# The key transposes of causal linear attention, at the start of the next eighth of a unit instead of the end of their own

## The chip, the cores and the metric

One Trainium2 chip, one of its cores. The metric is the device time of one execution in microseconds, the median of the runs. The program is one launch with three phases behind each other: the attention phase (with the token mixing ahead of it), an MLP phase with the router, and a phase of routed experts.

## What is computed

The reference takes x of 16 x 512 x 256 x 4. Cut to what matters here:

```
h = einsum('bhid,oi,od->bho', x, weighted_sum, weight)      # token mixing
z = layernorm(h)
# attention on z, 16 heads of 64, causal and linear:
q, k = elu((ln(z) @ wq) @ proj) + 1, elu((ln(z) @ wk) @ proj) + 1;  v = ln(z) @ wv
for t: kv += k_t v_t^T; ksum += k_t; out_t = (q_t kv) / (q_t ksum + 1e-6)
z = z + out @ wo;  z = z + gelu(ln(z) @ w1 + b1) @ w2 + b2;  h = h + z
h = h + mixture_of_experts(layernorm(h))                     # 8 routed, 1 shared
```

The change touches only the scan over t, in the attention phase.

## The kernel before

Each of the 16 images has 512 tokens. They are worked on in two **units** of 256 tokens, and each unit in two **chunks** of 128 tokens (`c` from 0 to 3 over an image). A chunk takes four **eighths** of a unit, one for each group `g` of four heads; an eighth is called by its number `s` from 0 to 7, and `s` 0 to 3 are chunk 2h, 4 to 7 chunk 2h + 1 of half h. All matrix products are done in two halves of fp16 (a high part and the rest), which is why so many steps come as "make the high part, then the low part".

Causal attention is done by chunks: within a chunk the scores of 128 x 128 are made, masked and multiplied with the values (`scores`, `scores_split`, `outputs`); over the chunks before, the running sum `kvacc` of k v^T is used (`kvh`, `kvl`). To add a chunk to that sum its keys must be turned, with the token on the partition. This is the step `keys(i, c, part)`, with `part` 0 and 1 for eight heads each. It runs for chunks 0 to 2; chunk 3 is the last and its sum is not needed.

- On TensorE `keys` is eight transposes (L645) from `ks` into the PSUM bank `pT`.
- On VectorE it is one copy (L917) of `pT` into `kt`, 128 x 1024 fp16.
- The other engines have nothing to do in it, and it issues no DMA.

The same bank `pT` takes the transposes of the attention's output, step `turn` (L705), four transposes that ScalarE then copies to `ot` (L803). The uses of `pT` follow each other strictly: each waits on the semaphore `turn_read` until the one before has been copied out. For chunk c the order is keys part 0, `turn` of group 0, keys part 1, `turn` of groups 1, 2, 3. `sums(i, c, g)` (L691, L692) multiplies `kt` with the values, and VectorE adds the result to `kvacc`.

There is no scheduler. One function `run`, called once for each engine with that engine's own steps, goes through the same list of steps, and each engine takes from it what it has. So the order of the calls in `unit` is the order on every engine. An eighth is made of: `outputs` of its group; the `turn` of an earlier group; the `scores` of a later one; and blocks of dense work from the table `DENSE`, of which the `early` ones stand ahead of `outputs` and the `late` ones behind it. A dense block "f" is eight heads' features (L550 to L552 into `pF`, then ScalarE's two activations L775 and L779, VectorE's `z` L876 and `hi` L881, GpSimd's `lo` L972, which together are the step `phi`), "v" a block of values (`vh` L785 on ScalarE, `vl` L886 on VectorE), "p" the output projection. At `s` = 2 the steps `x0` and `normed` of the unit after the next stand at the beginning: on VectorE L852, two of L863 and two `nl` (L869), on ScalarE L761 and L766; TensorE has no part in them. The last two units have no such unit ahead.

In the kernel before, `keys` of part 0 is called in eighth g = 1 behind `sums`, and part 1 in eighth g = 2, also behind `sums`, both ahead of `scores_split` (VectorE's `sl`, L909, in odd eighths) and ahead of the late `phi`.

Of the kernel before, what the change touches and what calls it, by code (L numbers as in the profile page):

```python
# [24 lines left out]
CH = 4  # L25
# [39 lines left out]
def after(u, n):  # L65

    return u[0] + (u[1] + n) // 2, (u[1] + n) % 2
# [27 lines left out]
def attention_phase(nc, io, w1_w, w2_w, mlp_loaded):  # L95
# [4 lines left out]
    with ExitStack() as ctx:  # L100
# [228 lines left out]
        def run(engine, steps):  # L329


            def step(name, *args):
                if name in steps:
                    steps[name](*args)

            def use(u, what, bank, before):


                kind, n = what
                if kind == "p":  # L340
                    step("project", after(u, -1), bank, before)
                elif kind == "f":
                    step("features", after(u, 1), n, bank, before)
                else:
                    step("values", after(u, 1), n, bank, before)

            def finish(u, what, bank):
                if what[0] == "f":
                    step("phi", after(u, 1), what[1], bank)
                elif what[0] == "p":  # L350
                    step("project_read", after(u, -1), bank)
                    step("residual", after(u, -1))

            def real(u):
                return u[0] < SEQS

            def mixed(u, k):
                step("mix", u, k)
                if k == XS - 1:
                    step("h", u)  # L360

            def normed(u):
                step("mean", u)
                step("centre", u)
                step("var", u)
                step("rstd", u)
                step("x0", u)
                step("normed", u)

            def dense(turn, first, last):  # L370


                slots, n = [], turn % 2
                before = {n: ("v", VALS - 2, 1), 1 - n: ("v", VALS - 1, 1)}
                for s in range(8):
                    uses = [], []
                    for place, (kind, k) in enumerate(DENSE[s]):
                        if not ((kind == "p" and first) or (kind != "p" and last)):
                            uses[place].append(((kind, k), n % 2, before[n % 2]))
                            before[n % 2] = (kind, k, 0)  # L380
                        n += 1
                    slots.append(uses)
                return slots

            def unit(u, start=False, last=False):


                i, h = u
                slots = dense(h, start, last)
                ahead, far = after(u, 2), after(u, 3)  # L390
                for s in range(8):
                    c, g = 2 * h + s // 4, s % 4
                    early, late = slots[s]

                    summed = (c, g - 2) if g >= 2 and c < CH - 1 else (c - 1, g + 2) if g < 2 and c > 0 else None

                    if g < 2:
                        quad = (i, c, g + 2)
                    elif c < CH - 1:
                        quad = (i, c + 1, g - 2)  # L400
                    else:
                        quad = None if last else (i + 1, 0, g - 2)
                    if s == 2 and real(ahead):
                        step("x0", ahead)
                        step("normed", ahead)
                    for what in early:
                        use(u, *what)
                    step("outputs", i, c, g)

                    if g >= 2:  # L410
                        step("turn", i, c, g - 2)
                    elif c > 0:
                        step("turn", i, c - 1, g + 2)
                    elif not start:
                        step("turn", i - 1, CH - 1, g + 2)
                    for what in early:
                        finish(u, *what[:2])
                    if quad is not None:
                        step("scores", *quad)
                    step("outputs_split", i, c, g)  # L420
                    if s == 1 and real(ahead):
                        step("var", ahead)
                        step("rstd", ahead)
                    for what in late:
                        use(u, *what)
                    if summed is not None:
                        step("sums", i, *summed)
                    if g in (1, 2) and c < CH - 1:
                        step("keys", i, c, g - 1)
                    if quad is not None:  # L430
                        step("scores_split", *quad)
                    if summed is not None:
                        step("sums_split", i, *summed)
                    if s == 0 and real(ahead):
                        step("mean", ahead)
                        step("centre", ahead)
                    if 1 <= s <= XS and real(far):
                        step("split", far, s - 1)
                    if s >= 4 and real(far):
                        mixed(far, s - 4)  # L440
                    for what in late:
                        finish(u, *what[:2])

            for k in range(XS):
                step("split", (0, 0), k)
                mixed((0, 0), k)
            normed((0, 0))
            for k in range(XS):
                step("split", (0, 1), k)
            slots = dense(-1, True, False)  # L450
            for s in range(8):
                for what, bank_no, before in slots[s][0] + slots[s][1]:
                    use((0, -1), what, bank_no, before)
                    finish((0, -1), what, bank_no)
                if s < XS:
                    mixed((0, 1), s)
                elif s == 4:
                    normed((0, 1))
            for k in range(XS):
                step("split", (1, 0), k)  # L460
                mixed((1, 0), k)
            for q in range(2):
                step("scores", 0, 0, q)
                step("scores_split", 0, 0, q)
            unit((0, 0), start=True)
            unit((0, 1))
            for i in range(1, SEQS - 1):
                unit((i, 0))
                unit((i, 1))
            unit((SEQS - 1, 0))  # L470
            unit((SEQS - 1, 1), last=True)
            step("turn", SEQS - 1, CH - 1, 2)
            step("turn", SEQS - 1, CH - 1, 3)
            step("project", (SEQS - 1, 1), LAST_BANK, ("p", 0, 1))
            step("project_read", (SEQS - 1, 1), LAST_BANK)
            step("residual", (SEQS - 1, 1))
# [1721 lines left out]
```

## Time and profile before

| | us |
|---|---|
| median of 3 runs | 2622.9 (2621.56 to 2630.17) |
| the profiled execution | 2629.9 |
| its span | 2628.2 |
| TensorE busy | 2258.0 (86%) |
| VectorE busy | 1783.4 (68%) |
| ScalarE busy | 1525.8 (58%) |
| GpSimd busy | 1468.2 (56%) |
| mean granted clock of TensorE | 0.946 of full |

The span is the profiled execution's own, from its first to its last instruction. Busy time is the time in which at least one instruction of the engine runs. The attention phase takes the first 1500 us or so. Matmuls overlap in the rows, so a matmul's duration is more than the distance to the next one: a row of 0.27 us may stand 0.11 us behind the last.

### The profile page before, as it was taken

How to read it: one execution, taken by the hardware profiler on the slowest of the kernel's cores; microseconds unless marked ns; L12 is line 12 of the kernel's file. 1: busy time of each engine (PE TensorE's matmuls, PEld its weight loads, DVE VectorE, ACT ScalarE, POOL GpSimd, SP SyncE). 2: the span in 40 equal slices, each digit the busy share in tenths (PEclk: the TensorE clock that was granted, in tenths of full speed). 3: DMA queues.
4: the chain of work that ended last, by engine and by line, in shares of the span. 5: the costliest groups of instructions: out<-in, count | busy, mean ns of one | idle time of the engine just before them, and what ended most of it. 6: DMA issues, size and time to landing. Idle time of an engine off the chain costs nothing. (4 is left out here: it accounts for less than half of the span.)

```text
span 2628.2 us, 64033 instructions
## 1 busy us (share of the span) xinstructions
PE 2258.0 (86%) x24112; PEld 1738.2 (66%) x24112; DVE 1783.4 (68%) x3983; ACT 1525.8 (58%) x2890; POOL 1468.2 (56%) x1449
## 2 busy tenths in 40 slices
PE   3799999999999999999999858989998999894774
PEld 2588787878787887878787736555555555552553
DVE  2477778777777777777777746766776677664442
ACT  3576777767777777677677645544554455441232
POOL 1376666666666756666666621553454345436576
PEclk8899999999999999999999979999999999997887
DMA  3344444444444434444443330111111111000775
GB/s 109 101 129 126 108 123 128 123 117 123 125 116 123 115 97 114 100 105 105 114 102 90 82 107 33 57 52 54 42 57 66 40 35 46 27 21 17 156 141 71
DMA packets 310913, 236.32 MB, mean 90 GB/s; under 512 B 28057, under 2 KB 275853, under 8 KB 310608
## 3 DMA queue, kind: packets, MB, share of 16 engines
q1 hardware_dynamic: 274352, 197.25, 28.1%
q0 software_dynamic: 23808, 21.74, 4.7%
q10 hardware_dynamic: 12448, 13.24, 1.6%
q8 instruction: 194, 3.18, 0.5%
q14 instruction: 111, 0.91, 0.1%
HBM read 73.32 MB, written 82.58 MB: 59 GB/s over the span
## 5 line engine op out<-in xcount | busy, mean ns | idle before, releaser
L1857 POOL DMA_INDIRECT slot_dram<-xt,slot_u x256 | 267.4, 1045 | 77.1 <-issue 77.1
L550 PE MATMUL pF<-nh,qk_h 128*128 128x256 f16 x1024 | 281.7, 275 | 7.8 <-DVE nl L869 4.4
L551 PE MATMUL pF<-nh,qk_l 128*128 128x256 f16 x1024 | 281.5, 275 | 0.0
L552 PE MATMUL pF<-nl,qk_h 128*128 128x256 f16 x1024 | 281.3, 275 | 0.0
L972 POOL TENSOR_TENSOR lo<-z,hi 128x512 f16<-128x512 f32 x128 | 148.6, 1161 | 198.6 <-DVE hi L881 198.6
L1845 POOL TENSOR_TENSOR xt<-xn,xt 128x512 f16<-128x512 f32 x32 | 40.0, 1269 | 330.5 <-ACT xt L1528 330.5
L796 ACT ACTIVATE sh<-sm 128x512 f16<-128x512 f32 x256 | 160.0, 625 | 88.2 <-DVE sm L902 82.5
L984 POOL TENSOR_TENSOR ol<-on,oh 128x256 f16<-128x256 f32 x256 | 172.2, 673 | 69.5 <-ACT oh L819 69.5
L876 DVE SCALAR_TENSOR_TENSOR z<-pF,z 128x512 f32<-128x512 f32 x256 | 175.1, 684 | 41.6 <-ACT z L779 39.0
L972 POOL TENSOR_TENSOR w_w<-z,hi 128x512 f16<-128x512 f32 x128 | 157.7, 1232 | 60.4 <-DVE hi L881 60.4
L991 POOL TENSOR_TENSOR kvl<-kvacc,kvh 128x260 f16<-128x260 f32 x192 | 157.9, 822 | 50.3 <-ACT kvh L827 50.3
L902 DVE TENSOR_TENSOR sm<-pS,mask 128x512 f32<-128x512 f32 x256 | 174.4, 681 | 10.1 <-PE pS L636 10.1
L1309 PE MATMUL pY<-w_h,gh 128*128 128x256 f16 x512 | 154.5, 302 | 30.0 <-issue 29.8
L550 PE MATMUL pO<-vh,sh 128*128 128x65 f16 x1024 | 119.4, 193 | 67.7 <-issue 48.1
L881 DVE CAST hi<-z 128x512 f16<-128x512 f32 x256 | 170.5, 666 | 8.8
L775 ACT ACTIVATE z<-pF 128x512 f32<-128x512 f32 x256 | 149.9, 586 | 45.1 <-PE pF L552 42.9
L966 POOL TENSOR_TENSOR xl<-w_w,xh 128x512 f16<-128x512 f32 x128 | 148.0, 1159 | 47.3 <-ACT xh L726 47.3
L1311 PE MATMUL pY<-w_l,gh 128*128 128x256 f16 x512 | 154.1, 301 | 22.4 <-issue 22.0
L1310 PE MATMUL pY<-w_h,gl 128*128 128x256 f16 x512 | 154.6, 302 | 18.6 <-issue 18.4
L803 ACT ACTIVATE ot<-pT 128x512 f16<-128x512 f16 x256 | 149.8, 585 | 31.0 <-PE pT L705 30.3
L779 ACT ACTIVATE z<-z 128x512 f32<-128x512 f32 x256 | 161.3, 630 | 8.2
L2107 POOL DMA_INDIRECT out_rows<-yb,xg x80 | 126.7, 1584 | 61.4 <-ACT yb L2052 35.9
(299 smaller groups left out, 8517.1 us busy)
## 6 DMA issues: line engine op xcount, KB each, us to landing
w_w<-in_x SPq DMA_DIRECT2D x128, 256.0 KB, 3.0
qdh<-hi SPq DMA_DIRECT2D x256, 128.0 KB, 2.7
qdl<-lo SPq DMA_DIRECT2D x256, 128.0 KB, 2.8
ks<-hi SPq DMA_DIRECT2D x128, 128.0 KB, 3.1
ks<-w_w SPq DMA_DIRECT2D x128, 128.0 KB, 3.1
slot_dram<-blank ACTq DMA_DIRECT2D x8, 1360.0 KB, 6.7
xg<-slot_dram SPq DMA_DIRECT2D x40, 272.0 KB, 2.9
x_dram<-x SPq DMA_DIRECT2D x32, 256.0 KB, 2.2
```

The source lines that it names most:

```text
L550: pe.matmul(out, wh, mh, start=first, stop=False, skip_group_check=True)
L551: pe.matmul(out, wl, mh, start=False, stop=False, skip_group_check=True)
L552: return pe.matmul(out, wh, ml, start=False, stop=last, skip_group_check=True)
L779: nc.scalar.activation(z[:, s, :, :], z[:, s, :, :], ACT.Exp, scale=-1.0, bias=-math.log(PHI_DOWN)).then_inc(e_ready, 1)
L796: nc.scalar.activation(sh[:, q, :, :], sm[:, n % 2, :, :], ACT.Copy).then_inc(sh_ready, 1)
L876: nc.vector.scalar_tensor_tensor(z[:, s, :, :], pF[bank_no][:, :].rearrange("p (b n) -> p b n", b=2), 0.0, z[:, s, :, :], ALU.max, ALU.add ...
L881: nc.vector.tensor_copy(hi[:, n % MOVES, :, :], z[:, s, :, :]).then_inc(fh_ready, 1)
L902: nc.vector.tensor_tensor(sm[:, n % 2, :, :], pS[:, :].rearrange("p (a b) -> p a b", b=P), mask[:, :].unsqueeze(1).broadcast_to([P, 4, P]) ...
L972: nc.gpsimd.tensor_tensor(lo[n % MOVES // 2][:, n % 2, :, :], z[:, units(w, FEATS, n) % ZS, :, :], hi[:, n % MOVES, :, :], ALU.subtract).t ...
L984: nc.gpsimd.tensor_tensor(ol[:, n % 2, :], on[:, n % 2, :, :].rearrange("p a b -> p (a b)"), oh[:, n % 2, :], ALU.subtract).then_inc(ol_re ...
L991: nc.gpsimd.tensor_tensor(kvl[:, heads, :], kvacc[:, heads, :], kvh[:, heads, :], ALU.subtract).then_inc(kvl_ready, 1)
L1857: nc.gpsimd.indirect_dma_start(io["slot_dram"], bass.IndirectOffsetOnAxis(slot_u[:, i % XT, c, k:k + 1], 0), xt[:, i % XT, c, :], None, bo ...
```

## The change

The two calls of `keys` move. Part 0, called at the end of eighth g = 1, is now called at the beginning of eighth g = 2, and part 1 at the beginning of g = 3 instead of the end of g = 2. In both cases the new place is behind `x0` and `normed`, where these are called.

```diff
                     if s == 2 and real(ahead):
                         step("x0", ahead)
                         step("normed", ahead)
+
+                    if g >= 2 and c < CH - 1:
+                        step("keys", i, c, g - 2)
                     for what in early:
                         use(u, *what)
                     step("outputs", i, c, g)
...
                     if summed is not None:
                         step("sums", i, *summed)
-                    if g in (1, 2) and c < CH - 1:
-                        step("keys", i, c, g - 1)
                     if quad is not None:
                         step("scores_split", *quad)
```

The order of the uses of `pT` stays as it was, and so do all semaphore counts. Lines behind the second place are one higher in the changed file (L917 becomes L918, L705 becomes L706).

VectorE's queue, at the end of eighth 1 and the first part of eighth 2 of a unit in the middle, before:

```order
L917 COPY kt<-pT 128x1024 [waits kv_done,turned]
L909 TENSOR_TENSOR sl<-sm,sh 128x512 [waits sh_ready]
L876 SCALAR_TENSOR_TENSOR z<-pF,z 128x512 [waits e_ready]
L881 CAST hi<-z 128x512 [waits moved_k,f_ready]
L852 TENSOR_TENSOR x<-w_w 128x512 [waits x1_stored,hx_ready1,xc_ready,rs_step]
L863 SCALAR_TENSOR_TENSOR w_w<-x,g,r 128x256 [waits nh_ready,nl_ready,x0_ready,rs_step]
L863 SCALAR_TENSOR_TENSOR w_w<-x,g,r 128x256
L869 SCALAR_TENSOR_TENSOR nl<-w_w,b,nh 128x256 [waits nh_ready,tn_ready] x2
L926 TENSOR_SCALAR dn<-pO 128x4 [waits o_done]
```

and after the change:

```order
L910 TENSOR_TENSOR sl<-sm,sh 128x512 [waits sh_ready]
L877 SCALAR_TENSOR_TENSOR z<-pF,z 128x512 [waits e_ready]
L882 CAST hi<-z 128x512 [waits moved_k,f_ready]
L853 TENSOR_TENSOR x<-w_w 128x512 [waits x1_stored,hx_ready1,xc_ready,rs_step]
L864 SCALAR_TENSOR_TENSOR w_w<-x,g,r 128x256 [waits nh_ready,nl_ready,x0_ready,rs_step]
L864 SCALAR_TENSOR_TENSOR w_w<-x,g,r 128x256
L870 SCALAR_TENSOR_TENSOR nl<-w_w,b,nh 128x256 [waits nh_ready,tn_ready] x2
L918 COPY kt<-pT 128x1024 [waits kv_done,turned]
L927 TENSOR_SCALAR dn<-pO 128x4 [waits o_done]
```

The copy `kt` of part 0 has moved past seven other instructions, from ahead of `sl` to behind `nl`.

The same queue at the end of eighth 2 and the start of eighth 3, before:

```order
L947 COPY kvacc<-pKV 128x260 [waits kvl_ready,kvh_ready,kv_done]
L917 COPY kt<-pT 128x1024 [waits kv_done,turned]
L876 SCALAR_TENSOR_TENSOR z<-pF,z 128x512 [waits e_ready]
L881 CAST hi<-z 128x512 [waits moved_k,f_ready]
L886 SCALAR_TENSOR_TENSOR vl<-pF,vh 128x8x64 [waits vh_ready]
```

and after the change:

```order
L948 COPY kvacc<-pKV 128x260 [waits kvl_ready,kvh_ready,kv_done]
L877 SCALAR_TENSOR_TENSOR z<-pF,z 128x512 [waits e_ready]
L882 CAST hi<-z 128x512 [waits moved_k,f_ready]
L918 COPY kt<-pT 128x1024 [waits kv_done,turned]
L887 SCALAR_TENSOR_TENSOR vl<-pF,vh 128x8x64 [waits vh_ready]
```

The copy of part 1 has moved behind the late feature block's `z` and `hi`.

And VectorE's queue at the end of eighth 5 and the start of eighth 6, in chunk 1 of an image, before:

```order
L917 COPY kt<-pT 128x1024 [waits kv_done,turned]
L909 TENSOR_TENSOR sl<-sm,sh 128x512 [waits sh_ready]
L876 SCALAR_TENSOR_TENSOR z<-pF,z 128x512 [waits e_ready]
L881 CAST hi<-z 128x512 [waits moved_k,f_ready]
L926 TENSOR_SCALAR dn<-pO 128x4 [waits o_done]
```

and after the change:

```order
L910 TENSOR_TENSOR sl<-sm,sh 128x512 [waits sh_ready]
L877 SCALAR_TENSOR_TENSOR z<-pF,z 128x512 [waits e_ready]
L882 CAST hi<-z 128x512 [waits moved_k,f_ready]
L918 COPY kt<-pT 128x1024 [waits kv_done,turned]
L927 TENSOR_SCALAR dn<-pO 128x4 [waits o_done]
```

Here it has moved behind `sl`, `z` and `hi`.

On TensorE the transposes keep their place between the same matmuls, except in eighths 5 and 6 of a unit with chunks 0 and 1: there the twelve matmuls of a step of token mixing (`mix`, L550 to L552 into `pM`), which stood behind the transposes, now stand ahead of them.

## Rows read from the trace of the kernel before

**Rows 1.** Busy time by engine (instructions), granted clock, DMA share, GB/s, steady part.
```profile
core 0: us, PE busy (x) PEld busy (x) DVE busy (x) ACT busy (x) POOL busy (x), PEclk, DMA share, GB/s
400.00:1400.00 1000.00, 931.93 (x12423) 798.17 (x12422) 773.68 (x1601) 710.73 (x1444) 659.42 (x691) 1.00 0.44 114
```
**Rows 2.** TensorE's waits, 400 to 1400 us: for whom, us in total, times, longest.
```profile
PE pO L550 <- issue: 35.4, 23, 1.8
PE pT L645 <- ACT ot L803: 24.6, 22, 1.5
PE pO L550 <- DVE sl L909: 7.1, 22, 0.7
```
**Rows 3.** Timeline of TensorE: start us, us, line, out<-in, count [idle before <-releaser].
```profile
711.67 0.27 PE L705 MATMUL pT<-ident,oh 128*128 128x128 f16 x2
...
713.54 0.27 PE L552 MATMUL pF<-nl,qk_h 128*128 128x256 f16 x1
...
715.20 0.62 PE L645 MATMUL pT<-ident,ks 128*128 128x128 f16 x8 [1.14 <-ACT ot L803]
715.85 0.39 PE L550 MATMUL pF<-wv_h,nh 128*128 128x512 f16 x1
...
717.89 0.27 PE L705 MATMUL pT<-ident,oh 128*128 128x128 f16 x2
...
719.63 0.38 PE L552 MATMUL pF<-wv_l,nh 128*128 128x512 f16 x1
...
723.38 0.19 PE L550 MATMUL pO<-vh,sh 128*128 128x65 f16 x1 [1.44 <-issue]
```
**Rows 4.** Timeline of VectorE in the same unit.
```profile
705.90 0.69 DVE L917 COPY kt<-pT 128x1024 f16<-128x1024 f16 x1
708.34 0.69 DVE L909 TENSOR_TENSOR sl<-sm,sh 128x512 f16<-128x512 f32 x1 [1.74 <-ACT sh L796]
...
713.57 0.88 DVE L869 SCALAR_TENSOR_TENSOR nl<-w_w,b,nh 128x256 f16<-128x256 f32 x2 [0.31 <-ACT nh L761]
714.37 0.15 DVE L926 TENSOR_SCALAR dn<-pO 128x4 f32<-128x4 f32 x1
...
717.24 0.68 DVE L876 SCALAR_TENSOR_TENSOR z<-pF,z 128x512 f32<-128x512 f32 x1
717.96 1.23 DVE L881 CAST hi<-z 128x512 f16<-128x512 f32 x1
...
721.50 0.69 DVE L886 SCALAR_TENSOR_TENSOR vl<-pF,vh 128x512 f16<-128x512 f32 x1 [0.37 <-ACT vh L785]
```
**Rows 5.** The tile `kt`: min/median/max ns, first and last start.
```profile
L917 DVE COPY kt<-pT x96: 672/682/693, 120.3 to 1512.3; 128x1024 f16<-128x1024 f16 x96
```
**Rows 6.** Timeline of ScalarE in the same unit.
```profile
714.57 0.58 ACT L803 ACTIVATE ot<-pT 128x512 f16<-128x512 f16 x1
...
715.55 0.58 ACT L775 ACTIVATE z<-pF 128x512 f32<-128x512 f32 x1
716.16 0.63 ACT L779 ACTIVATE z<-z 128x512 f32<-128x512 f32 x1
```
**Rows 7.** Timeline of VectorE in the unit before, eighths 5 to 7.
```profile
686.35 1.02 DVE L909 TENSOR_TENSOR sl<-sm,sh 128x512 f16<-128x512 f32 x1
...
688.01 0.43 DVE L881 CAST hi<-z 128x512 f16<-128x512 f32 x1
688.35 0.16 DVE L926 TENSOR_SCALAR dn<-pO 128x4 f32<-128x4 f32 x1
...
694.06 0.69 DVE L886 SCALAR_TENSOR_TENSOR vl<-pF,vh 128x512 f16<-128x512 f32 x1 [1.67 <-ACT vh L785]
```
**Rows 8.** Timeline of TensorE in that unit, eighth 6.
```profile
687.97 0.27 PE L705 MATMUL pT<-ident,oh 128*128 128x128 f16 x2
```
**Rows 9.** TensorE after a long wait, and the busy time behind it.
```profile
123.41 0.19 PE L550 MATMUL pO<-vh,sh 128*128 128x65 f16 x1 [3.12 <-DVE sl L909]
123.50:126.90 3.40, 3.40 (x32) 2.96 (x32) 3.23 (x5) 0.34 (x1) 2.26 (x2) 0.50 0.85 195
```

## The prediction

> **What bounds the kernel now.** The first view to read is the busy time of each engine over the steady part of the attention phase. From 400 to 1400 us TensorE is busy 932 of 1000 us at a granted clock of 1.00; VectorE has 774, ScalarE 711, GpSimd 659 [rows 1]. So TensorE is the bound, with some 68 us per 1000 of idle time, and what matters is what stops it. The waits of TensorE in the same window name it: 22 waits before the key transposes (L645) for ScalarE's copy `ot`, 24.6 us; 23 before the first score-times-value matmul (L550, `pO`), 35.4 us, which the view can't attribute; and 22 short ones for `sl` [rows 2]. That is one of each large kind in every unit (half image; 22 or 23 units lie in the window). Everything I forecast is per unit, so one unit is replayed: the one whose eighth 1 ends at 705 us.
>
> TensorE's rows there [rows 3]: the output transposes at 711.67, the eighth's feature matmuls end at 713.81 (713.54 + 0.27), then after the sums 1.14 us of idle until the key transposes of part 1 at 715.20; value matmuls at 715.85; the next output transposes at 717.89; the last value matmul of eighth 3 ends at 720.01 (719.63 + 0.38); 1.44 us idle before 723.38.
>
> VectorE's rows [rows 4]: the copy `kt` (part 0) at 705.90, 0.69 us. Behind it VectorE is idle 1.74 us, until ScalarE has made `sh`, and only then `sl` starts at 708.34. From there it runs nearly solid: the normalisation of a later unit ends with two `nl` from 713.57 (0.88 us, up to 714.45), `dn` at 714.37, then, with `kt` of part 1 just ahead of it, `z` 717.24, `hi` 717.96, `vl` 721.50. So before `sl` VectorE has time to give away, and from 708.34 to 723 it has hardly any. That decides the case.
>
> **The change, part by part.** It adds and removes no instruction: 768 transposes and 96 `kt` copies stay. No DMA is issued by the step, and SP, ScalarE and GpSimd have no part in it, so their queues keep their order. What moves is the place in the queues of TensorE and VectorE.
>
> On TensorE the place is the same at the boundary of eighths 1 and 2 and of 2 and 3: nothing of TensorE stands between the end of one eighth and the start of the next. Only in eighths 5 and 6 (chunk 1 of an image) twelve mixing matmuls come ahead of the transposes instead of behind them. They are work either way: cost nil.
>
> On VectorE `kt` moves much further. It goes behind `sl`, the late `phi` pair (`z`, `hi`), and, at eighth 2, behind the whole of `x0` and `normed`, which are called ahead of the new place. And TensorE's next output transposes wait for that copy, since they write the same bank `pT`: there is a queue of one between them.
>
> *Step 1, `kt` of part 0 at eighth 2.* Taking it from 705.90 frees 0.69 us where VectorE then idles 1.74 us for `sh` [rows 4], so `sl` stays at 708.34 and the rest of that chain too: gain nil. It now stands where `dn` stood, at 714.37, and ends 0.68 to 0.69 later, 715.06 (the 96 copies took 0.672 to 0.693 us [rows 5]). TensorE reaches the output transposes at 711.67, as now, and gets them at 715.1: **a new wait of 3.4 us**. Behind them on TensorE, which issues in order, stand the scores, a feature block, the sums, the key transposes and the values.
>
> *Step 2, the old wait goes.* TensorE is through with the sums 1.14 us ahead of 715.20, at 714.06, 2.39 us behind the start of the output transposes, so the key transposes of part 1 come at 715.1 + 2.4 = 717.5. By then ScalarE has long copied `ot`: its own normalisation ends where `ot` began, 714.57 [rows 6], and the copy takes 0.58 from the end of the transposes at 715.5. The wait of 1.14 us disappears; TensorE is at 717.5 against 715.20, 2.3 us late.
>
> *Step 3, `kt` of part 1 at eighth 3.* Now it stands behind `z` and `hi` of the late feature block. That block ends 2.14 us after the output transposes (711.67 to 713.81), at 717.2. ScalarE's two activations take 0.58 and 0.63 [rows 6], so 718.5; `z` on VectorE 0.72 until `hi` may start (717.24 to 717.96 [rows 4]), 719.3; `hi` takes 1.23 us at this place [rows 4] but 0.43 in a quieter one [rows 7]. `kt` then ends between 720.5 and 721.2. Values follow the key transposes by 0.65 and the output transposes follow the values by 2.04 [rows 3], so TensorE stands ready at 717.5 + 0.65 + 2.04 = 720.2 and waits 0.3 to 1.0 us more. I take 721.2, by the row of the very same `hi`, since GpSimd's `sl`, whose neighbour `hi` is, waits for ScalarE as `hi` does and moves with it. Against 717.89 TensorE is 3.3 us late (2.5 with the short `hi`: 720.4).
>
> *Step 4, up to the next rendezvous.* The last value matmul ends 2.12 us behind the output transposes (717.89 to 720.01), so 723.3; ScalarE's `vh`, as large as its `z`, takes 0.58 [rows 6] and `vl` follows, 723.95 against 721.50 now. From `vl` to the matmul at 723.38 is 1.88 us [rows 3, 4], so that one comes at 725.85: **2.5 us late**, 1.7 with the short `hi`. TensorE's own work gives less (5.49 us from 717.89 to 723.38 less 1.44 idle is 4.05; 721.2 + 4.05 = 725.25), so this chain is the last. Behind it VectorE has gaps again and nothing makes up for the delay.
>
> The normalisation stands in eighth 2 of 30 of the 32 units (the last two have none ahead): 30 x 2.5 = **75 us**, at the low end 30 x 1.7 = 51.
>
> *Step 5, chunk 1 of each image (eighths 5 to 7).* At eighth 6 `kt` takes the place of `dn`, 688.35, right behind `hi` [rows 7], and ends at 689.04; TensorE was at the output transposes at 687.97 [rows 8]: 1.1 us of wait. What VectorE can gain by the removed copy is the time in which `sl` followed it, between 0 and some 0.6 us (`sl` at 686.35 [rows 7]); at eighth 1 `sl` waits for ScalarE's `sh` anyway, so I take little, 0.15, and the wait as 0.95 us, 16 times: **15 us**, with 0.5 x 16 = 8 and 1.1 x 16 = 18 as ends. TensorE has no wait for the rest of this unit in which the delay could be made good. The second `kt` of the chunk falls where VectorE idles 1.67 us (`vl` at 694.06 [rows 7]): nil.
>
> *Step 6, TensorE's clock.* The steady part runs at 1.00 with waits of up to 1.8 us [rows 1, 2]. The trace has one wait near the new length: 3.12 us that ended at 123.41, and in the 3.4 us behind it the granted clock was 0.50, that is 1.2 GHz [rows 9]. The new wait is 3.4 us. Behind it stand the 2.1 us of scores and features on which step 3 hangs. 3.4 us at half rate do 1.7 us of work less. From both sides: nothing if the clock stays, 1.7 per unit if it falls every time once, up to 2.1 if all the work ahead of `z` runs at half rate. I take 1.5, nearer to the one row that has such a wait: 30 x 1.5 = **45 us**, ends 0 and 63.
>
> One page was weighed for step 1. The nearest row for a VectorE copy that moves among GpSimd's work is `hi`, 0.43 against 1.23 us [rows 4, 7]; the `kt` copies lie between 0.672 and 0.693 wherever they stand [rows 5]. The Trainium skill, page "VectorE: DVE Perf Modes", section "Why PSUM operands drop a tier", says that a copy out of PSUM can't use both SBUF read ports, and its section "Two Vector instructions with no wait between them" that the second of these is shared with GpSimd; by that, `kt`, which reads PSUM, does not swell, and the trace agrees (0.69). Were it to swell like `hi`, step 1 would be 0.8 us longer per unit, 24 us in all.
>
> **The sum.** 75 + 15 + 45 = 135 us. The profiled execution took 2629.9 us with a span of 2628.2, so it would become 2765; the median of the runs is 2622.9, 7 lower, and the forecast for it is 2622.9 + 135, some **2758 us**.
>
> **The rivals.**
> (a) The waits come, the clock holds. For it: it never left 1.00 in the steady part. Against it: [rows 9]. 90 us more, 2713.
> (b) The clock falls for twice as long, since the waits of steps 3 and 4 follow some 6 and 11 us behind: 30 x 3 for step 6, 2803. For it: nothing in the steady part shows how fast it comes back after a second wait.
> (c) Hidden. VectorE reaches `kt` in time because the chain ahead of it starts 0.6 us earlier without the old copy. The 1.74 us of idle before `sl` speak against it, and 0.6 would not cover 3.4. 2623.
> (d) Faster. The old wait for `ot` (1.14 us, 32 times, 36 us) goes and no new one comes, 2587. That needs `kt` to end by 711.67, that is the normalisation 3.4 us earlier; a gain begins only once the new wait is below 1.1 us. `x0` and the normalisation sit behind `hi` and ScalarE, neither of which changes.
> (e) The change doesn't move `kt` past `normed`: excluded by the order of the built program, which has it between `nl` and `dn`.
>
> **How the numbers follow.** Forecast 0.57, (a) 0.22, (b) 0.13, (c) 0.05, (d) 0.03. The range: the low end takes (a) with the low ends of step 4 and 5, halfway, 2695 (75 down to 51 and 15 down to 8 would make 2682); the high end leaves the far half of (b), 2795. Within 0.3% of 2622.9 is about what a measurement of this kernel can't tell from no change; (c) is that case, 0.05, (d) the faster one, 0.03, and the rest, 0.92, is slower.
>
> **What would show each step.** In the changed kernel's waits of TensorE a new group stands on top: output transposes (one line on, L706) for `kt`, some 30 of 3.4 us, 30 near 1.0 and 16 near 1.0, about 150 us in all, and the group "key transposes for `ot`" is gone. VectorE idles longer before `sl` at eighth 1 (2.3 us). The granted clock from 400 to 1400 us is below 1.00, near 0.95; if it is 1.00, step 6 is wrong and (a) holds. If the time from one image to the next grows by 5.6 us (90 / 16) where the clock holds, steps 1 to 5 are right. I am wrong if `kt` at eighth 2 doesn't start right behind `nl`, or if the wait at 723.38 absorbs more than the 0.8 us of the delay that step 4 lets it (3.3 down to 2.5).

## Result and profile after

The changed kernel takes 2762.1 us (median of 4 runs, 2756.33 to 2763.01), the kernel before 2622.9: the ratio is 1.052, with a 95% interval of 1.0496 to 1.0544, so it is 139 us slower. The forecast was 2758. One of the four runs of the kernel with `nh` and `nl` around eighth 7 took 12801 us and is left out of its numbers below.

The runs of this study were made in groups, on several chips, and the kernel before took 2622.9, 2610.3 or 2502.5 to 2502.9 us in them; each comparison below is with the kernel before in the same group. This difference between groups lies behind the attention phase, so one more number is used that compares all of them: the start of the first scatter of the MLP phase (GpSimd's first write of `slot_dram`), which is the end of the attention phase plus a stretch that the change doesn't touch. It stands at 1647.3 us before and 1781.9 us after, so 134.6 us are made in the attention phase. Behind it the two profiled executions differ the other way, 980.9 us before and 972.7 after; the profiled executions took 2629.9 us, near the top of that kernel's runs, and 2756.3, the lowest of the other's (2765 was forecast for it). In a second profile of the changed kernel, in another group, the scatter stands at 1781.8. The rows are those of the tile `slot_dram` (min/median/max ns, first and last start), before and after:

```profile
L1857 POOL DMA_INDIRECT slot_dram<-xt,slot_u x256: 978/981/1383, 1647.3 to 2424.5; - x128
```
```profile
L1858 POOL DMA_INDIRECT slot_dram<-xt,slot_u x256: 978/980/1383, 1781.9 to 2552.5; - x128
```

The busy time of the engines in the steady part, after (columns as in [rows 1]), and TensorE's waits there (as [rows 2]):

```profile
core 0: us, PE busy (x) PEld busy (x) DVE busy (x) ACT busy (x) POOL busy (x), PEclk, DMA share, GB/s
400.00:1400.00 1000.00, 880.37 (x11333) 749.88 (x11332) 712.74 (x1458) 652.87 (x1313) 597.41 (x626) 0.97 0.40 104
```
```profile
PE pT L706 <- DVE kt L918: 100.9, 50, 3.6
PE pO L551 <- issue: 11.7, 20, 0.6
PE pO L551 <- DVE sl L910: 7.0, 21, 0.7
```

TensorE has 120 us of idle time per 1000 instead of 68, and its clock has left 1.00. The wait for `ot` [rows 2] is gone, and the unattributed one fell from 35.4 to 11.7 us. In their place stand 50 waits of the output transposes for `kt`, 100.9 us. Over the whole run they are 78 waits and 153.4 us, where the prediction had some 76 and 150.

One unit of the changed kernel in which the clock held, TensorE (timeline, columns as in [rows 3]):

```profile
771.54 0.28 PE L706 MATMUL pT<-ident,oh 128*128 128x128 f16 x2 [3.27 <-DVE kt L918]
...
773.42 0.27 PE L553 MATMUL pF<-nl,qk_h 128*128 128x256 f16 x1
...
773.78 0.61 PE L646 MATMUL pT<-ident,ks 128*128 128x128 f16 x8
...
777.69 0.29 PE L706 MATMUL pT<-ident,oh 128*128 128x128 f16 x2 [1.27 <-DVE kt L918]
...
782.33 0.19 PE L551 MATMUL pO<-vh,sh 128*128 128x65 f16 x1 [0.59 <-issue]
```

and VectorE beside it, which answers to [rows 4]:

```profile
764.77 0.69 DVE L910 TENSOR_TENSOR sl<-sm,sh 128x512 f16<-128x512 f32 x1 [2.44 <-ACT sh L797]
...
770.00 0.88 DVE L870 SCALAR_TENSOR_TENSOR nl<-w_w,b,nh 128x256 f16<-128x256 f32 x2 [0.31 <-ACT nh L762]
770.80 0.68 DVE L918 COPY kt<-pT 128x1024 f16<-128x1024 f16 x1
...
775.02 0.69 DVE L877 SCALAR_TENSOR_TENSOR z<-pF,z 128x512 f32<-128x512 f32 x1 [0.62 <-ACT z L780]
775.75 1.28 DVE L882 CAST hi<-z 128x512 f16<-128x512 f32 x1
776.95 0.68 DVE L918 COPY kt<-pT 128x1024 f16<-128x1024 f16 x1
777.55 0.68 DVE L887 SCALAR_TENSOR_TENSOR vl<-pF,vh 128x512 f16<-128x512 f32 x1
```

Read the two together. `kt` of part 0 starts at 770.80, right behind the `nl` pair, ends at 771.48, and TensorE goes on at 771.54 after 3.27 us. The idle time before `sl` grew from 1.74 to 2.44 us: the 0.7 us that the old copy took there were given away for nothing. The second `kt` ends at 777.63, TensorE goes on at 777.69 after 1.27 us. The key transposes (773.78) wait for nobody now.

### The profile page after: what moved, and what is told of

It is laid out like the page before. It is cut to its first block and busy times, and to the rows that moved or that the text cites. A ratio compares the mean times of both kernels' runs of the same rounds, so it can differ in the third digit from the quotient of the medians.

```text
span 2754.6 us, 64033 instructions
## 1 busy us (share of the span) xinstructions
PE 2299.7 (83%) x24112; PEld 1768.9 (64%) x24112; DVE 1795.4 (65%) x3983; ACT 1534.4 (56%) x2890; POOL 1467.7 (53%) x1449
## 5 line engine op out<-in xcount | busy, mean ns | idle before, releaser
L551 PE MATMUL pF<-nh,qk_h 128*128 128x256 f16 x1024 | 292.4, 286 | 8.6 <-DVE nl L870 4.4
L552 PE MATMUL pF<-nh,qk_l 128*128 128x256 f16 x1024 | 291.7, 285 | 0.0
L553 PE MATMUL pF<-nl,qk_h 128*128 128x256 f16 x1024 | 291.3, 284 | 0.0
L706 PE MATMUL pT<-ident,oh 128*128 128x128 f16 x512 | 73.7, 227 | 155.0 <-DVE kt L918 153.4
L979 POOL TENSOR_TENSOR sl<-sm,sh 128x512 f16<-128x512 f32 x128 | 148.3, 1158 | 69.8 <-ACT sh L797 69.6
L910 DVE TENSOR_TENSOR sl<-sm,sh 128x512 f16<-128x512 f32 x128 | 104.4, 816 | 106.0 <-ACT sh L797 106.0
L967 POOL TENSOR_TENSOR xl<-w_w,xh 128x512 f16<-128x512 f32 x128 | 147.7, 1157 | 47.4 <-ACT xh L727 47.4
```

The source lines that it names most:

```text
L551: pe.matmul(out, wh, mh, start=first, stop=False, skip_group_check=True)
L552: pe.matmul(out, wl, mh, start=False, stop=False, skip_group_check=True)
L553: return pe.matmul(out, wh, ml, start=False, stop=last, skip_group_check=True)
```

## Experiments

Each kernel is an edit of `unit`'s list of steps or of one engine's steps. "Scatter" is the start of the first scatter less 1647.3. The time from one image to the next is the distance of two like waits of TensorE some 90 us apart, near 700 to 900 us; where the clock falls it varies by a microsecond or so.

| kernel | ratio to before (95%) | us over before | scatter | image to image |
|---|---|---|---|---|
| before | 1 | 0 | 0 | 90.04 |
| changed | 1.052 (1.0496 to 1.0544) | +139 | +134.6 | 98.28, 99.35 |
| changed, again | 1.0518 (1.0501 to 1.0536) | +135.2 | +134.5 | |
| part 0 alone | 1.0398 (1.0381 to 1.0416) | +101.0 | +101.3 | 97.11 |
| part 1 alone | 1.0024 (1.0013 to 1.0035) | +5.3 | +4.4 | 90.08 |
| ahead of x0 and normed | 1.0158 (1.0142 to 1.0175) | +39.8 | +39.0 | 92.30 |
| changed, wait filled | 1.0396 (1.0379 to 1.0414) | +98.6 | +100.3 | 96.41 |
| changed, chunk 1 as before | 1.0435 (1.0418 to 1.0453) | +113.4 | +110.8 | 97.49 |
| before, normed at eighth 4 | 1.0126 (1.0109 to 1.0143) | +33.3 | +32.7 | 92.26 |
| before, x0 and normed at 4 | 1.0195 (1.0178 to 1.0212) | +51.7 | +49.8 | 93.35 |
| before, nh and nl around eighth 7 | 1.0246 (1.0223 to 1.0269) | +62.0 | +60.7 | 93.47 |
| before, all but x0 at eighth 7 | 1.0314 (1.0293 to 1.0336) | +81.1 | +79.2 | 95.41 |
| before, L863 at eighths 5 and 7 | 1.0242 (1.0223 to 1.0261) | +62.5 | +63.4 | 94.76 |
| before, nh and nl at start of eighth 7 | **0.9898** (0.9881 to 0.9914) | **-25.6** | -24.6 | 88.12 |

### Part 0 alone

```diff
                         step("normed", ahead)
+                    if g == 2 and c < CH - 1:
+                        step("keys", i, c, 0)
...
-                    if g in (1, 2) and c < CH - 1:
-                        step("keys", i, c, g - 1)
+                    if g == 2 and c < CH - 1:
+                        step("keys", i, c, 1)
```

> Only part 0 of the key transposes is moved to the start of the next eighth; part 1 stays at the end of its own. My theory (the copy kt stands behind the normalisation on VectorE, TensorE's output transposes wait for it): the wait of 3.3 us at eighth 2 stays whole, the ones at eighth 3 go, because kt of part 1 falls where VectorE waits for ScalarE. By the same replay as in the prediction the unit is 1.3 us late instead of 2.5, so 30 x 1.3 + 15 + 45 for the clock = 99 us over the kernel before, about 2722, and the clock still falls once in most units. Rival (each of the two moves costs by its own, half each): 2692.

Measured: 2603.6 against 2502.5, 101 us more; expected were 99. TensorE's waits from 400 to 1400 us:

```profile
PE pT L707 <- DVE kt L919: 78.0, 31, 3.6
```

31 waits instead of 50: the 3.3 us ones and those of chunk 1 are left, those at eighth 3 are gone. The granted clock there is 0.97, as in the changed kernel. Part 0 alone makes three quarters of the loss.

### Part 1 alone

```diff
                         step("normed", ahead)
+                    if g == 3 and c < CH - 1:
+                        step("keys", i, c, 1)
...
-                    if g in (1, 2) and c < CH - 1:
-                        step("keys", i, c, g - 1)
+                    if g == 1 and c < CH - 1:
+                        step("keys", i, c, 0)
```

> Only part 1 is moved. My theory: no wait of 3 us anywhere, so the clock stays at 1.00 in the steady part and the old wait for ot stays too, now at the start of eighth 3. kt of part 1 stands behind hi, TensorE waits 0.9 to 1.9 us for it, and VectorE's own chain, which has the same work in it, gives most of it back by the next wait: 0 to 1.1 us per unit, 2623 to 2656, I take 2641. Rival (half each): 2692.

Measured: 5.3 us more, at the low end of the 0 to 33 expected. The waits:

```profile
PE pT L647 <- ACT ot L805: 24.5, 22, 1.5
PE pT L707 <- DVE kt L919: 19.8, 23, 1.0
PE pO L552 <- issue: 13.6, 23, 0.8
```

The wait for `ot` is where it was [rows 2], a wait for `kt` of 0.67 to 1.03 us is new, and the one behind it fell from 35.4 to 13.6 us: what TensorE loses at eighth 3 it gets back at eighth 4, since VectorE's queue has the same work in it up to there. The two moves together cost 139 us, the sum of the two alone is 106: behind a late part 0, part 1 has no such slack.

### Both, ahead of x0 and normed

```diff
+                    if g >= 2 and c < CH - 1:
+                        step("keys", i, c, g - 2)
                     if s == 2 and real(ahead):
                         step("x0", ahead)
                         step("normed", ahead)
-
-                    if g >= 2 and c < CH - 1:
-                        step("keys", i, c, g - 2)
```

> Both parts at the start of the next eighth, but called ahead of x0 and normed instead of behind them. On TensorE this is the very same order as the changed kernel. My theory: kt of part 0 then ends at about 711.6 in the replayed unit, when TensorE reaches the output transposes at 711.67, so the wait of 3.3 us goes and with it the falls of the clock; left are the waits at eighths 3 and 6. 30 x (0.5 to 1.3) + 15 = 30 to 54 us over before, about 2665. Rival (the cost comes from where TensorE's transposes stand, or from the mixing matmuls that they changed places with): no different from the changed kernel, 2762.

Measured: 39.8 us more (expected 30 to 54). TensorE has the very order of the changed kernel, and 99 us of the 139 are gone. So it is not the place of the transposes on TensorE that costs; it is that `kt` stands behind the normalisation on VectorE.

```profile
PE pT L646 <- ACT ot L804: 36.3, 22, 2.0
PE pT L706 <- DVE kt L918: 28.4, 32, 1.0
PE pO L551 <- issue: 12.9, 22, 0.6
```

No wait is longer than 2 us, and the granted clock from 400 to 1400 us is 1.00 to two places; it fell once, behind a wait of 1.99 us (rows in the last section).

### The wait filled with matmuls

The output's values are not touched: the fillers write columns that nobody reads.

```diff
+FILL = 28
...
                     step("outputs", i, c, g)
+                    if s == 2 and real(ahead):
+                        step("fill", i, c, g)
...
+            def fill(i, c, g):
+                for k in range(FILL):
+                    pe.matmul(pKV[:, 4 * VW:512], qk_h[:, 0, 0:P], qk_l[:, 0, 0:512 - 4 * VW], start=True, stop=True,
+                              skip_group_check=True)
```

> The changed kernel with 28 more matmuls of 252 columns, into columns of a PSUM bank that nobody reads, right ahead of the output transposes of eighth 2 (30 units). They are 3.0 us of work and fit into the wait of 3.3 us, so they add nothing by themselves; they keep TensorE busy. If step 6 of the prediction holds (the falls of the clock cost some 45 of the 139 us), the clock stays at 1.00 from 400 to 1400 us and the time is about 2717. If the clock's falls cost nothing, since TensorE waits for others anyway, it stays at 2762; if the fillers are in the way, above that.

```profile
702.19 3.17 PE L689 MATMUL pKV<-qk_l,qk_h 128*128 128x252 f16 x28
705.66 0.29 PE L714 MATMUL pT<-ident,oh 128*128 128x128 f16 x2 [0.29 <-DVE kt L926]
```
```profile
400.00:1400.00 1000.00, 935.11 (x12181) 802.29 (x12182) 729.61 (x1495) 671.13 (x1352) 614.26 (x643) 1.00 0.42 106
```

Measured: 98.6 us over before, where the changed kernel is 135 to 139. The 28 matmuls fill the wait to 0.29 us and add nothing; the clock is back at 1.00. By the start of the scatter the difference is 134.6 - 100.3 = 34 us: that is what the clock's falls behind these waits cost, shown by a kernel that does more work and is faster.

### The changed kernel again, and with chunk 1 as before

```diff
-                    if g >= 2 and c < CH - 1:
+                    if g >= 2 and c in (0, 2):
                         step("keys", i, c, g - 2)
...
                         step("sums", i, *summed)
+                    if g in (1, 2) and c == 1:
+                        step("keys", i, c, g - 1)
```

> The changed kernel itself, beside the experiments on their own chip, where the kernel before takes some 2502 us. What stands in the attention phase is the same there, so 139 us over before, about 2641. If it is less by some 40, the clock's falls (which the fillers took away in the experiment before) are not the same on this chip.

> The changed kernel, but with the key transposes of chunk 1 of every image where they were (end of their own eighth); chunks 0 and 2 stay moved. Step 5 of the prediction: 15 us less than the changed kernel, since the wait of 0.97 us at eighth 6 goes, 16 times. Rival: another wait of that half takes its place, 0 us less.

Measured: 135.2 us over before for the changed kernel, 113.4 for the other, 21.8 us less where 15 were expected. The next section measures the step itself at 1.1 us an image, 18 us. The other 4 us are not shown to have a cause; the clock falls at other places in this kernel (mean 0.97 in both).

### Moving the normalisation instead

All experiments so far say that VectorE's queue of eighths 2 and 3 is what TensorE waits for. If so, taking the normalisation out of it should make the kernel before faster. The first attempt moved `normed` from eighth 2 to eighth 4:

```diff
                     if s == 2 and real(ahead):
                         step("x0", ahead)
+                    if s == 4 and real(ahead):
                         step("normed", ahead)
```

> The kernel before, with normed of the later unit called at the start of eighth 4 instead of eighth 2 (x0 stays). It touches no key transpose. If it is the normalisation on VectorE and ScalarE that makes the chain of eighths 2 and 3 late, both waits of the kernel before (1.14 us for ot, 1.44 us ahead of the first score-value matmul) go: 30 x 2.6 = 78 us faster, less what the normalisation costs at its new place, where VectorE idles some 2.2 us of the 2.5 that it needs: about 2435, 2425 to 2460. Rival: the waits come from VectorE's total work and turn up again in eighths 4 to 6: 2502.

Measured: 33 us slower, where 68 us faster were expected. Both theories were off. The two waits per unit did shrink: from the output transposes of eighth 2 to the first score-value matmul of eighth 4 TensorE takes 9.6 us (725.15 to 734.78) instead of 11.7 (711.67 to 723.38). But more came back behind it:

```profile
734.78 0.19 PE L551 MATMUL pO<-vh,sh 128*128 128x65 f16 x1 [0.89 <-issue]
739.76 0.28 PE L706 MATMUL pT<-ident,oh 128*128 128x128 f16 x2 [0.20 <-ACT ot L804]
741.06 0.23 PE L636 MATMUL pS<-qdh,ks 128*128 128x128 f16 x1 [0.90 <-DVE sm L903]
748.12 0.19 PE L551 MATMUL pO<-vh,sh 128*128 128x65 f16 x1 [1.84 <-DVE sl L910]
```

From 734.78 to 748.12 are 13.34 us; the same stretch before is 723.38 to 733.55, 10.17. VectorE's side shows why:

```profile
734.49 2.25 DVE L864 SCALAR_TENSOR_TENSOR w_w<-x,g,r 128x256 f32<-128x256 f32 x2
736.67 0.47 DVE L870 SCALAR_TENSOR_TENSOR nl<-w_w,b,nh 128x256 f16<-128x256 f32 x1
737.39 0.48 DVE L870 SCALAR_TENSOR_TENSOR nl<-w_w,b,nh 128x256 f16<-128x256 f32 x1 [0.25 <-ACT nh L762]
737.79 0.15 DVE L927 TENSOR_SCALAR dn<-pO 128x4 f32<-128x4 f32 x1
```

The normalisation now stands ahead of `dn`, and takes 3.3 us there, since the pair L864 takes 2.25 us where GpSimd works beside both of them, instead of 1.59 where it works beside one. VectorE's idle time ahead of `dn` at eighth 4 was no room: it is the time that TensorE takes to make what `dn` reads, and the scores and the outputs hang on what follows.

> As the experiment with normed at eighth 4, but with x0 moved there too. Theory: the same waits are gone, and 0.7 us more of VectorE's work is put where it has 2.2 us of idle time, so it is equal to or up to 10 us slower than with normed alone: about 2440. Rival (total work): 2502.

Measured: 51.7 us slower, so 18 more for the 0.7 us of x0 in 30 units: at that place nearly all of it is on the path (30 x 0.7 = 21).

The next three put the work at eighth 7, where VectorE idles 1.85 us ahead of `vl`. For them `normed` was cut into its parts: `tn` (VectorE's two L863), `nh` (ScalarE), `nl` (VectorE) and `hb` (ScalarE's two `hT`). In each, `nl` and `hT` were called at the end of that eighth and `nh` at its start; the first left the two L863 at eighth 2, the second took them to eighth 7, the third one of them to eighth 5.

```diff
                         step("x0", ahead)
-                        step("normed", ahead)
+                        step("tn", ahead, (0, 1))
+                    if s == 7 and real(ahead):
+                        step("nh", ahead)
...
                         finish(u, *what[:2])
+                    if s == 7 and real(ahead):
+                        step("nl", ahead)
+                        step("hb", ahead)
```

> The kernel before with the last part of the normalisation (ScalarE's two nh and two hT, VectorE's two nl) taken from eighth 2 to eighth 7; the two L863 stay at eighth 2. The experiment with all of it at eighth 4 showed that VectorE's idle time ahead of dn is no room, since the score and output chain hangs on dn and sm; at eighth 7 the idle 1.7 to 1.85 us stands ahead of vl, on which nobody waits soon. Theory: ot is copied at once, the wait of 1.14 us goes, VectorE's chain is 1.1 us shorter: 30 x 1.1 = 33 us faster than the kernel before, ratio 0.987. Rival (any later place costs TensorE more than it gives, as at eighth 4): 1.00 or slower.

> The two L863 are moved to eighth 7 too; only x0 stays at eighth 2. If the gain goes on with the work that is taken out of eighth 2, 2.06 us per unit (as far as eighth 4, which the experiment with normed at eighth 4 showed) less some 0.5 us where L863 is longer than VectorE's idle 1.85 us at eighth 7: 30 x 1.5 = 45 us faster, ratio 0.983. Rival: at eighth 7 the L863 pair takes 2.25 us beside GpSimd, as it did at eighth 4, and vl comes late for eighth 0 of the next unit: between 0 and 20 us faster.

> As the one before, with the first L863 at eighth 5 and the second at eighth 7. Theory: the first one falls into 1.44 us of idle time ahead of dn, of which it takes 0.8 to 1.1, so no wait comes of it, and the second fits into eighth 7: 30 x 1.9 = 57 us faster, ratio 0.978. Rival: what is ahead of dn delays it as at eighth 4, so slower than with all at eighth 7.

Measured: 62, 81 and 62 us slower, where 33, 45 and 57 us faster were expected; the rivals failed too, but for the first one's, which had it slower. The wait for `ot` was gone, as expected, and a larger one stood at eighth 0 of the next unit. Timeline of the first of the three, VectorE and then TensorE:

```profile
766.58 0.88 DVE L882 SCALAR_TENSOR_TENSOR nl<-w_w,b,nh 128x256 f16<-128x256 f32 x2
767.56 0.27 PE L555 MATMUL pF<-nh,qk_h 128*128 128x256 f16 x1 [2.27 <-issue]
```

The matmul at 767.56 is the first of the feature block at eighth 0 of the next unit, which reads `nh` and `nl`, and the two `nl` end at 767.46. What I had overlooked is that the deadline of `nl` is the start of that eighth for TensorE, which runs ahead of VectorE; the end of eighth 7 in VectorE's queue is too late. The clock was 0.97 in all three.

That gave the last one: `nl` at the start of eighth 7, ahead of `vl`, and `hT` in ScalarE's gap of 1.4 us at eighth 3.

```diff
                         step("x0", ahead)
-                        step("normed", ahead)
+                        step("tn", ahead, (0, 1))
+                    if s == 7 and real(ahead):
+                        step("nh", ahead)
+                        step("nl", ahead)
...
                         step("turn", i - 1, CH - 1, g + 2)
+                    if s == 3 and real(ahead):
+                        step("hb", ahead)
```

> The kernel before, with nh and nl called at the start of eighth 7 (in the experiment with nl at its end TensorE stood 2.3 to 2.5 us at eighth 0 of the next unit, whose first feature block needs nl, and the clock fell there) and the two hT called in eighth 3 between ScalarE's ot and oh, where it idles 1.44 us. The two L863 stay at eighth 2. Theory: VectorE's two nl and ScalarE's nh fall into the 1.85 us in which VectorE waits ahead of vl at eighth 7, so no new wait comes; the wait of 1.14 us for ot goes and VectorE's chain of eighths 2 and 3 is 1.2 us shorter (measured with nl at the end of eighth 7: 10.5 us from the output transposes to the first score-value matmul of eighth 4, against 11.7). 30 x 1.2 = 36 us faster than the kernel before, ratio 0.986. Rival: TensorE is bound by the length of VectorE's queue as a whole and the 1.2 us come back in eighths 4 to 7 or at eighth 0: ratio 1.00 or above.

Measured: 2477.1 against 2502.7, ratio 0.9898, 25.6 us faster than the kernel before, and so faster than both kernels of this case. The steady part's waits and busy time:

```profile
PE pO L555 <- issue: 33.6, 22, 1.7
PE pO L555 <- DVE sl L926: 11.8, 22, 1.1
PE pF L555 <- DVE x L910: 2.4, 11, 0.4
```
```profile
400.00:1400.00 1000.00, 951.86 (x12731) 818.53 (x12729) 806.51 (x1634) 725.25 (x1476) 675.67 (x704) 1.00 0.45 115
```
```profile
721.43 1.78 DVE L882 SCALAR_TENSOR_TENSOR nl<-w_w,b,nh 128x256 f16<-128x256 f32 x2 [0.57 <-ACT nh L766]
723.14 0.68 DVE L903 SCALAR_TENSOR_TENSOR vl<-pF,vh 128x512 f16<-128x512 f32 x1
```

TensorE is busy 952 of 1000 us, against 932 [rows 1]. The wait for `ot` (24.6 us [rows 2]) is gone and nothing of its size has come. It is 10 us less than expected. The two `nl` take 1.78 us at eighth 7 where they took 0.88 at eighth 2 [rows 4], and the wait for `sl` grew from 7.1 to 11.8 us; that these make up the 10 us was not tested. At the end of the phase, from 1430 to 1505 us, the granted clock fell four times; before it did not fall from 170 us until 1516.

## Why the prediction was right

- **Steps 1 and 2 (part 0 behind the normalisation).** Forecast: a wait of 3.4 us, the old one of 1.14 gone. Measured: 3.13 to 3.31 us in 25 of the 29 places where it is over 3 us, the old one gone. From the output transposes to the key transposes it was 773.78 - 771.54 = 2.24 us where I had written 2.39; this lay off the path, since TensorE waits again at the next output transposes.
- **Step 3 (part 1 behind `hi`).** Forecast 0.3 to 1.0 us, 1.0 taken. Measured 1.27 (777.69), with `hi` at 1.28, and 1.64 in the units of the other kind (told under step 4), which the replay of one unit did not cover. From one output transposes to the next it was 6.15 us (771.54 to 777.69); the forecast was 6.1 (715.1 to 721.2). So `kt` came as forecast, and the wait is longer because TensorE came earlier: by the 0.15 us of the line above, and because the values follow the key transposes by 0.44 us, not by 0.65 as in [rows 3].
- **Step 4.** Forecast 2.5 us per unit. The matmuls of the mean (L574, one group per unit) give a unit's length, here without and with a fall of the clock, after the change:

```profile
755.57 0.46 PE L574 MATMUL pM<-hT,ones 128*128 128x256 f32 x1
...
803.11 0.44 PE L574 MATMUL pM<-hT,ones 128*128 128x256 f32 x1
...
853.49 0.46 PE L574 MATMUL pM<-hT,ones 128*128 128x256 f32 x1
...
902.46 0.43 PE L574 MATMUL pM<-hT,ones 128*128 128x256 f32 x1
```

  Two kinds of unit alternate, since a unit is half an image and only one half has chunk 1's keys. Before they last 44.8 and 45.2 us. With the wait filled, where the clock stays at 1.00, they last 47.4 and 48.9 in all but the first and a few, so 2.6 and 3.7 us more. 2.6 is step 4, 0.1 above the forecast. An image takes 6.3 us more where the clock holds; the prediction had named 5.6 as the sign.
- **Step 5 (chunk 1).** Forecast 0.95 us per image, measured 3.7 - 2.6 = 1.1: the mis-sized term is the 0.15 us that I let VectorE gain. VectorE gains nothing: `sl` now waits for `sh`, so it starts only 0.14 us earlier against the output transposes, and then takes 1.19 us instead of 1.02:

```profile
741.49 1.19 DVE L910 TENSOR_TENSOR sl<-sm,sh 128x512 f16<-128x512 f32 x1 [0.36 <-ACT sh L797]
...
743.65 0.68 DVE L918 COPY kt<-pT 128x1024 f16<-128x1024 f16 x1
...
744.39 0.29 PE L706 MATMUL pT<-ident,oh 128*128 128x128 f16 x2 [0.97 <-DVE kt L918]
```

- **Step 6 (the clock).** Forecast 45 us, ends 0 and 63; measured 34, by the filled kernel. The mechanism is right and the size was a third too large. In the changed kernel the granted clock fell behind 24 of the 29 waits of over 3 us, so not in each unit. The unit from 755.57 to 803.11 has a wait of 3.27 us and no fall and lasts 47.54; the one from 853.49 to 902.46 has a wait of 3.15 us and a fall and lasts 48.97. So a fall costs some 1.4 us, and 24 x 1.4 = 34. After two waits of nearly the same length (3.27 and 3.30 us), in the unit without a fall and in one with it:

```profile
771.60:775.00 3.40, 3.40 (x44) 2.88 (x45) 2.21 (x5) 2.13 (x5) 1.90 (x2) 1.00 0.23 79
818.30:821.60 3.30, 3.30 (x23) 2.73 (x24) 1.88 (x4) 0.90 (x2) 1.90 (x2) 0.53 0.22 79
```

  TensorE got through 44 matmuls in the first and 23 in the second, at 2.4 GHz and mostly 1.2 GHz.
- **The sum.** 135 was the forecast, 75 + 15 + 45. Measured by the scatter: 100 + 34 = 134.6, of which the 100 answer to 75 + 15. The two errors, +10 and -11, cancel, so that the total came out within 1% is luck. Of the +10, steps 4 and 5 explain 5 (30 x 2.55 + 16 x 1.14 = 95); the rest is not in the units of the steady part and was not traced. The medians are 139 apart in this group and 135.2 in the second; what lies behind the attention phase differs by some us from run to run and was not looked into.
- **The rivals.** (a) falls with the clock of 0.97; (b) falls: from 170 to 1500 us 19 stretches of half clock lasted 3.4 us and 4 lasted 6.8; (c) and (d) fall with the waits. That `kt` in itself, and not the transposes on TensorE, is the cause was argued in the prediction and is shown by the kernel with both ahead of x0 and normed.
- **`kt` beside GpSimd.** It did not swell, as was weighed: the 96 copies take 675 to 693 ns in the changed kernel. From 400 to 1400 us, 20 of them ran beside an idle GpSimd (681 to 684 ns) and 30 beside one that was busy all the while (676 to 693). `hi`, which reads no PSUM, took 426 to 428 ns beside an idle GpSimd and 1274 to 1283 beside a busy one.

## What to carry to other kernels

Before a step is moved in a list that several engines share, look at what it is moved past on each of them: here TensorE's queue was all but the same, and VectorE's had seven more instructions ahead of a copy that TensorE waits for with everything it does next. Idle time is room only if nothing that others wait for stands right behind it; of the six kernels that moved parts of the normalisation into idle time, one was faster. Deadlines are those of the engine that reads, and it may run an eighth ahead.

## What the hardware showed beyond that

Waits of 3.1 to 3.3 us in an otherwise busy TensorE were followed by a granted clock of 0.50 in most cases and not in all; work without use, put into the wait, saved 34 us. The kernel with `nh` and `nl` around eighth 7 had waits of 2.3 to 2.5 us and a clock of 0.97 too. Waits of up to 1.8 us were not followed by a fall in the kernel before or with `normed` at eighth 4, from 400 to 1400 us. A wait of 1.99 us was, in the kernel with the keys ahead of x0 and normed (the wait, and the window behind it):

```profile
960.52 0.62 PE L646 MATMUL pT<-ident,ks 128*128 128x128 f16 x8 [1.99 <-ACT ot L804]
961.50:964.90 3.40, 3.40 (x26) 2.11 (x25) 2.97 (x7) 2.73 (x6) 3.40 (x4) 0.50 0.44 154
```

The kernel before differed by 120 us between groups of runs, and not in the attention phase: from the scatter to the end are 980.9 us before and 853.6 in the kernel with part 1 alone. Whether it is the chip is not shown: the groups in which the kernel before took 2610.3 and 2502.7 us carry the same chip number. In the MLP phase of the first group the matmuls into `pY` have idle time ahead of them that nothing in the profile explains, and in the group of 2502.5 us they have none (groups by line from 1600 to 2400 us, the kernel before, and the like of its first row from part 1 alone):

```profile
L1309 PE MATMUL pY<-w_h,gh 128*128 128x256 f16 x480 | 145.8, 304 | 30.0 <-issue 29.8
L1310 PE MATMUL pY<-w_h,gl 128*128 128x256 f16 x480 | 145.9, 304 | 18.6 <-issue 18.4
L1311 PE MATMUL pY<-w_l,gh 128*128 128x256 f16 x480 | 145.4, 303 | 22.4 <-issue 22.0
```
```profile
L1311 PE MATMUL pY<-w_h,gh 128*128 128x256 f16 x480 | 130.9, 273 | 0.0
```

That is 71 us of idle time and, with it, longer matmuls, at a lower granted clock: 0.93 from 1579 to 2359 us in the one, 0.99 from 1583 to 2242 in the other. What makes the idle time was not settled.
